# Two PSUM banks for the turned probabilities, one for the values, and the value product last in each head

## The reference, cut to what matters

```python
# experts: each token sums the rows of its 8 experts
g = out_pad[eid, slot] * (w.reshape(-1) * valid.astype(w.dtype))[:, None]
y = jnp.zeros((T, Hd), x.dtype).at[tok].add(g)
...
# attention, per batch and head (4 x 16)
scores = jnp.einsum('bhtd,bhsd->bhts', q, k) / scale
attn = jax.nn.softmax(jnp.where(mask, scores, -jnp.inf), axis=-1)
out = jnp.einsum('bhts,bhsd->bhtd', attn, v)
return out.transpose(0, 2, 1, 3).reshape(B, T_text, N_HEADS * HEAD_DIM) @ Wo
...
# feed-forward, per batch
h = jax.nn.silu(bitlinear158(x, w1, b1))
h = jax.nn.gelu(h, approximate=False)
h = layer_norm(h, ln_g, ln_b)
return bitlinear158(h, w2, b2)
```

## Time and profile before

| | us |
|---|---|
| three runs | 549.42, 546.50, 547.52 |
| median | 547.52 |
| the profiled execution | 546.43 |
| its span from first to last instruction | 544.5 |
| slot loop, first `scores` to last `project` | 256.6 to 513.3 |
| tail behind it | 513.3 to 544.5 |
| busy over the span | PE 485.3 (89%), DVE 436.0 (80%), ACT 393.5 (72%), POOL 246.4 (45%) |

### The profile page before, as it was taken

The page is one execution under the profiler, slowest core; times in us unless marked ns, Lnnn a source line. Parts: engine busy times, 40 slices in busy tenths (PEclk is TensorE's granted clock), DMA queues, the critical chain, the costliest instruction groups (busy, mean ns, idle before and its releaser), DMA issues.

```text
span 544.5 us, 10844 instructions
## 1 busy us (share of the span) xinstructions
PE 485.3 (89%) x3402; PEld 399.9 (73%) x3402; DVE 436.0 (80%) x1213; ACT 393.5 (72%) x928; POOL 246.4 (45%) x255
## 2 busy tenths in 40 slices
PE   8958888799997999998999999987999889997925
PEld 6445555666787677777899999976999789986804
DVE  4889999999968487986668559869888699766887
ACT  2786777585374567886877777898687997798654
POOL 1139999894106656302772376125861232122121
PEclk9958999899999999998999999999899999999867
DMA  6655887572788997925220034001660000000000
GB/s 178 152 173 176 230 272 225 173 220 78 206 256 244 291 316 213 301 92 194 59 69 2 17 77 59 7 2 17 77 82 3 2 1 1 22 1 0 2 20 19
DMA packets 52558, 61.65 MB, mean 113 GB/s; under 512 B 6284, under 2 KB 42742, under 8 KB 52502
## 3 DMA queue, kind: packets, MB, share of 16 engines
q1 hardware_dynamic: 48662, 49.43, 30.5%
q0 software_dynamic: 3840, 11.54, 10.0%
HBM read 54.27 MB, written 6.69 MB: 112 GB/s over the span
## 4 chain that ended last, share of the span: by engine, by line
PE 49%; issue 17%; DVE 14%; ACT 12%; POOL 6%; DMA 2%; DVEq 0%; SPq 0%; ACTq 0%; POOLq 0%
PE ps L1712 8%; PE ps L1650 7%; PE ps L1651 6%; PE ps L1652 6%; DVE hst L1968 4%; PE ps L1701 4%; PE ps L1568 3%; PE ps L1370 2%; ACT pr L1085 2%; POOL dbu L636 2%; DVE hc L1980 2%; PE ps L1604 2%; PE ps L1589 2%; POOL G L683 1%; PE ps L1378 1%
## 5 line engine op out<-in xcount | busy, mean ns | idle before, releaser
L636 POOL TENSOR_TENSOR dbu<-du,brow 128x512 f32<-128x512 f32 x64 | 82.4, 1324 | 22.3 <-DVE du L1955 18.7
L721 POOL TENSOR_TENSOR pn<-pr,pinv 128x256 f32<-128x256 f32 x64 | 40.9, 639 | 107.8 <-DVE pinv L2376 107.3
L1712 PE MATMUL ps<-pT,cS 128*128 128x256 f32 x256 | 67.4, 386 | 0.0
L1085 ACT ACTIVATE pr<-ebuf,smin 128x256 f32<-128x256 f32 x128 | 63.6, 501 | 2.4 <-issue 1.8
L872 ACT ACTIVATE ps<-dtv,amat 128x510 f32<-128x510 f32 x64 | 44.0, 695 | 24.4 <-DVE hst L1968 19.5
L683 POOL DMA_INDIRECT G<-token_rows,idx_x x32 | 37.8, 1180 | 43.1 <-DVE wkv L2104 20.8
L705 POOL DMA_INDIRECT G<-expert_out,idx_g x48 | 50.9, 1061 | 11.5 <-issue 11.1
L2366 DVE CUSTOM_DVE_ANT_0 ebuf<-ps,mbias 128x256 f32<-128x256 f32 x128 | 49.0, 420 | 2.6 <-issue 2.6
L1650 PE MATMUL ps<-xnT,mqk 128*128 128x256 f32 x128 | 47.2, 368 | 4.3 <-DVE qT L2336 2.5
L1701 PE MATMUL ps<-ident,pn 128*128 128x128 f32 x256 | 39.5, 277 | 9.2 <-ACT pT L1100 5.0
L1712 PEld LDWEIGHTS ps<-pT,cS 128*128 128x128 f32 x256 | 44.8, 193 | 3.9
(11 more groups left out here) (387 smaller groups left out, 1486.2 us busy)
## 6 DMA issues: line engine op xcount, KB each, us to landing
brow<-state_rows SPq DMA_DIRECT2D x16, 512.0 KB, 4.0
wdn<-in_L_ffn_wd SPq DMA_DIRECT2D x12, 384.0 KB, 6.7
ebuf<-state_rows SPq DMA_DIRECT2D x17, 256.0 KB, 5.4
wgu<-in_L_ffn_wg SPq DMA_DIRECT2D x11, 384.0 KB, 5.3
wgu<-in_L_ffn_wu SPq DMA_DIRECT2D x11, 384.0 KB, 7.3
expert_out<-xn SPq DMA_DIRECT2D x11, 256.0 KB, 4.3
wo<-in_L_xattn_Wo SPq DMA_DIRECT2D x4, 512.0 KB, 5.8
wq<-in_L_xattn_Wq SPq DMA_DIRECT2D x4, 512.0 KB, 5.7
```

The source lines that it names most:

```text
L636: nc.gpsimd.tensor_tensor(dbu[:, j, :], du[:, j % 2, at:at + 512], brow[:, pair % BRING, j // 2, :], ALU.mult).then_inc(pool_dbu, 1)
L1085: last = A(pr[:, h % 2, tt, :], sneg[:, h % 2, tt, :], ACT.Exp, scale=-1.0, bias=smin[:, h % 2, tt:tt + 1], accum_out=psum_[:, h % 2, tt:t ...
L1712: last = pe.matmul(ps[:, 3 + 2 * (h % 2), 0:L], cS[:, b % 2, st, :], pT[:, h % 2, st, :], start=(st == 0), stop=(st == 1))
```

## The change

1. **Banks.** `turn_p` writes bank 4 for even heads and bank 5 for odd ones, and so waits for `turned_p` of two heads back instead of one. `values` writes one half or the other of bank 3, and so waits for `o_low` of the head just before it instead of two back.
2. **Order within a head.** On PE `values` goes behind `queries` and `project`, to the end of the slot. On ACT `o_high` goes behind `exps`. On DVE `o_low` goes behind `q_low`.
3. **Feed-forward.** `gelu` 1 is set apart from `gelu` 0: for f = 0 and 1 from at 13 (late) to at 14 (ACT's third place), for f = 2 from ahead of `q_high` to behind it. `squares` 1 of f = 0 and 1 goes behind `q_high`. `normal_hidden` 1 goes to the late place for f = 0 and 1, and `normal_hidden` 0 of f = 2 too.
4. **Gathers.** One at h = 0, two each at h = 1 to 7, one at h = 8.

```diff
@@ -434,6 +434,9 @@
         def query_out(i):
             return ps[:, 5 if i == 1 else 0, 0:L]
 
+        def values_out(h):
+            return ps[:, 3, L * (h % 2):L * (h % 2) + L]
+
         def cols(ap, a, b):
             return ap[:, a:b]
 
@@ -763,26 +766,28 @@
                 if b + 1 < B:
                     if h == 0:
                         gather(b + 1, 0, 0)
+                    if h == 1:
                         gather(b + 1, 0, 1)
                         gather(b + 1, 0, 2)
-                    if h == 1:
+                    if h == 2:
                         gather(b + 1, 0, 3)
                         gather(b + 1, 0, 4)
-                    if h == 2:
+                    if h == 3:
                         gather(b + 1, 0, 5)
-                    if h == 3:
                         gather(b + 1, 0, 6)
+                    if h == 4:
                         gather(b + 1, 0, 7)
-                    if h == 4:
                         gather(b + 1, 1, 0)
+                    if h == 5:
                         gather(b + 1, 1, 1)
+                        gather(b + 1, 1, 2)
                     if h == 6:
-                        gather(b + 1, 1, 2)
                         gather(b + 1, 1, 3)
                         gather(b + 1, 1, 4)
                     if h == 7:
                         gather(b + 1, 1, 5)
                         gather(b + 1, 1, 6)
+                    if h == 8:
                         gather(b + 1, 1, 7)
                     if h == 12:
                         root3(b + 1)
@@ -1097,13 +1102,13 @@
                 i = NH * b + h
                 act.wait_ge(pT_in_psum, i + 1)
                 wait_count(act, av_done, i - 1)
-                A(pT[:, h % 2].rearrange("p a b -> p (a b)"), bank(4), ACT.Copy).then_inc(pT_ready, 1)
+                A(pT[:, h % 2].rearrange("p a b -> p (a b)"), bank(4 + h % 2), ACT.Copy).then_inc(pT_ready, 1)
 
             def o_high(b, h):
                 i = NH * b + h
                 act.wait_ge(av_done, i + 1)
                 wait_count(act, o_added, i - 1)
-                A(oT[0][:, h % 2], bank(3 + 2 * (h % 2))[:, 0:L], ACT.Copy).then_inc(o_hi, 1)
+                A(oT[0][:, h % 2], values_out(h), ACT.Copy).then_inc(o_hi, 1)
 
             def preload(at, function):
 
@@ -1205,18 +1210,19 @@
                         silu(f, 1)
                     if at == 12 and f == B - 2:
                         gelu(f, 0)
-                        gelu(f, 1)
-                    if at == 18 and f < B - 2:
-                        squares(f, 1)
                     if at == 22 and f < B - 2:
                         turned_hidden(f, 0)
                     if at == (22 if f < B - 2 else 20):
                         turned_hidden(f, 1)
-                if 4 <= slot < NH * B + 4:
-                    o_high((slot - 4) // NH, (slot - 4) % NH)
                 if slot + 2 < NH * B:
                     q_high((slot + 2) // NH, (slot + 2) % NH)
                 for f, at in feeds(slot):
+                    if at == 14 and f < B - 2:
+                        gelu(f, 1)
+                    if at == 12 and f == B - 2:
+                        gelu(f, 1)
+                    if at == 18 and f < B - 2:
+                        squares(f, 1)
                     if at == 8 and f == B - 2:
                         turned(f)
                     if at == 13 and f == B - 2:
@@ -1231,6 +1237,8 @@
                     normal_half((slot - 1) // NH, (slot - 1) % NH)
                 if slot < NH * B:
                     exps(b, h)
+                if 4 <= slot < NH * B + 4:
+                    o_high((slot - 4) // NH, (slot - 4) % NH)
                 if slot == NH * B:
                     preload(1, ACT.Gelu)
                 if b + 1 < B:
@@ -1695,10 +1702,10 @@
                 i = NH * b + h
                 pe.wait_ge(p_ready, i + 1)
                 pe.wait_ge(p_half, i + 1)
-                wait_count(pe, pT_ready, i)
+                wait_count(pe, pT_ready, i - 1)
                 for st in range(2):
                     for tt in range(2):
-                        last = pe.transpose(ps[:, 4, L * st + P * tt:L * st + P * tt + P],
+                        last = pe.transpose(ps[:, 4 + h % 2, L * st + P * tt:L * st + P * tt + P],
                                             pn[:, h % 2, tt, P * st:P * st + P], ident[:])
                 last.then_inc(pT_in_psum, 1)
 
@@ -1707,9 +1714,9 @@
                 pe.wait_ge(pT_ready, i + 1)
                 if h == 0:
                     pe.wait_ge(rows_ready, b + 1)
-                wait_count(pe, o_ready, i - 1)
+                wait_count(pe, o_ready, i)
                 for st in range(2):
-                    last = pe.matmul(ps[:, 3 + 2 * (h % 2), 0:L], cS[:, b % 2, st, :], pT[:, h % 2, st, :], start=(st == 0),
+                    last = pe.matmul(values_out(h), cS[:, b % 2, st, :], pT[:, h % 2, st, :], start=(st == 0),
                                      stop=(st == 1))
                 last.then_inc(av_done, 1)
 
@@ -1826,12 +1833,12 @@
                 for f, at in feeds(slot):
                     if at == 9 and f == B - 2:
                         into(f, 0)
-                if 4 <= slot < NH * B + 4:
-                    values((slot - 4) // NH, (slot - 4) % NH)
                 if slot + 2 < NH * B:
                     queries((slot + 2) // NH, (slot + 2) % NH)
                 if 5 <= slot < NH * B + 5:
                     project((slot - 5) // NH, (slot - 5) % NH)
+                if 4 <= slot < NH * B + 4:
+                    values((slot - 4) // NH, (slot - 4) % NH)
                 if b + 1 < B:
                     if h == 13:
                         turn_xn3(b + 1)
@@ -2379,7 +2386,7 @@
                 i = NH * b + h
                 dve.wait_ge(o_hi, i + 1)
                 wait_count(dve, o_added, i - 1)
-                low(oT[1][:, h % 2], bank(3 + 2 * (h % 2))[:, 0:L], oT[0][:, h % 2], o_ready)
+                low(oT[1][:, h % 2], values_out(h), oT[0][:, h % 2], o_ready)
 
             def add_attention(b):
                 dve.wait_ge(o_added, NH * b + NH)
@@ -2743,10 +2750,8 @@
                         centred(f, 0)
                     if at == 15 and f == B - 2:
                         centred(f, 1)
-                    if at == (17 if f < B - 2 else 15):
+                    if at == 17 and f < B - 2:
                         normal_hidden(f, 0)
-                    if at == 17 and f < B - 2:
-                        normal_hidden(f, 1)
                     if at == (18 if f < B - 2 else 16):
                         largest(f, 0)
                     if at == 17 and f == B - 2:
@@ -2757,10 +2762,10 @@
                         scaled(f)
                     if at == 19 and f == B - 2:
                         scale_round(f, 1)
+                if slot + 2 < NH * B:
+                    q_low((slot + 2) // NH, (slot + 2) % NH)
                 if 4 <= slot < NH * B + 4:
                     o_low((slot - 4) // NH, (slot - 4) % NH)
-                if slot + 2 < NH * B:
-                    q_low((slot + 2) // NH, (slot + 2) % NH)
                 if b + 1 < B:
                     if h == 6:
                         add_choices(b + 1, 0, 0)
@@ -2793,6 +2798,8 @@
                         variance(f)
                         centred(f, 1)
                     if at == 15 and f == B - 2:
+                        normal_hidden(f, 0)
+                    if at == (17 if f < B - 2 else 15):
                         normal_hidden(f, 1)
                     if at == 18 and f < B - 2:
                         largest(f, 1)
```

## The result

| | us | ratio to before |
|---|---|---|
| before, median of 4 runs (546.50 to 549.42) | 547.49 | |
| after, median of 4 runs (563.73 to 567.92) | 565.36 | 1.0337, 95% interval 1.0305 to 1.0370 |
| forecast | 556.5 (549 to 562) | 1.016 |

A forecast was written before the change was run, and what follows sets the result against it. PE was taken to bound plain heads, and ACT the heads with feed-forward work from its gelu on. Terms 5.1 + 1.9 + 0.4 + 2.0 = 9.4 us on 546.43 gave 555.8, forecast as 556.5, range 549 to 562.

The forecast's parts named there:

- Plain heads at 3.43: Heads without feed-forward work stay at PE's own 3.43 us each, costed at nothing, with 0.7 us of cover for `project`.
- f = 1, +5.1: Slots 40 to 53 take 61.7 us instead of 56.65, from per-head rings summing to 59.0 plus 0.29, 0.86 and 1.56.
- The rings: One chain per head over ACT and DVE: `o_high`, `o_low`, reciprocal, mask, exponentials; 2.62 us, late DVE work added in full.
- f = 0, +1.9: Slots 24 to 37: same rings as f = 1, gathers hidden beneath them, set against 59.84 us.
- The 3.2 us between f = 0 and f = 1: 59.84 against 56.65 us for the same 14 slots, put down to gathers; slot 35 began 1.90 late on POOL's `pn`.
- Batch boundary, +0.4: At slot 14 `queries` waits 0.7 us instead of 0.3 for the next rows' low part; later two boundaries lie inside rings.
- the walk: Ring lengths added up slot by slot for f = 1 and from slot 60 on; chance 0.62 (552 to 559).
- Gathers too late for the sums, the last rival: A batch's last gather moves from slot 7 to 8; sums wanting it end slot 9, some 7 us on: hidden; no chance given.
- Two banks: Two banks for turned probabilities: all 5.0 us of `turn_p` waits on ACT's copy go, but turn into waits for `o_low`.
- End of the loop, +2.0: From slot 60 to the last `project`: 30.7 us instead of 28.7, by rings and the last three heads at 2.6 each.
- a rival for the mid-loop waits: Three PE waits over 3 us each bring a stretch at 1.2 GHz, +1 to +2 each: 559 to 562, chance 0.08.
- one doubt (what overlaps): Whether `project`'s waits overlap others: at best sum +2.6 (549 to 550); at worst none overlap, tail heads 3.4 each (+12).

The follow-up runs named there:

- the extra pass: One more DVE pass in slots 16 to 19, run in both kernels: slots 14 to 23 took 34.44 us before (34.44 without), 36.18 in the new (34.87 without).
- the two kernels of the last windows above: The kernel before (547.5 us), then it with gathers spread and new feed-forward places of f = 0 and 1 alone, old banks and order: 544.91 us, 0.9952.

## Why the prediction was right in direction and half in size

- *Plain heads at 3.43:* right, 3.44, and the extra pass shows how near the edge they are.
- *f = 1, +5.1:* +5.7, mostly as walked. The rings sum to 0.2 less than forecast, `add_attention` adds 0.86. The row for it was in the trace of before (0.74 us of DVE behind `q_low` at that slot) and has no term in the sum.
- *f = 0, +1.9:* +3.1. The same 0.86; two rings were 0.2 and 0.4 longer than in f = 1, the second by a pass of DVE that took 1.12 instead of 0.74. The 3.2 us between f = 0 and f = 1, put down to gathers, are not all theirs: with the gathers spread and the old order f = 0 still takes 1.2 longer.
- *Batch boundary, +0.4:* +0.4 in the stretch of slots 14 to 23, in part by luck. Slot 14 is 0.34 longer; slot 21, the first `project` of the batch, adds 0.23, and the other heads, at 3.41 instead of 3.43, give 0.14 back.
- *Slots 54 to 59, no term:* +0.4. Slot 57 took 5.92 instead of 5.39: late feed-forward work of f = 2 stands in the rings there too, and the walk began at slot 60.
- *Gathers too late for the sums, the last rival:* it was called hidden and is not quite. In slot 9 a sum waited 0.60 us for the last gathers, behind `o_low` and so in the ring:

```profile
288.68 1.29 DVE L2307 TENSOR_TENSOR G<-G 128x512 f32<-128x512 f32 x2 [0.60 <-DMA G<-expert_out,idx_g]
```

  The stretch of slots 6 to 13 is 0.7 longer; with the old order and the old banks the same wait was 1.03 us and cost nothing, but with the old order and the new banks (1.10 us) slot 11 took 3.97 instead of 3.43.
- *Two banks:* the rule on banks that the prediction set against its rings (the Trainium skill, PSUM — Partial Sum Buffer, Summary: rules for kernel authors) gives no gain here: 1.0024 alone. The wait for the copy was real, but PE then waited elsewhere: the 5.0 us gave way to 11.1 us of `values` waiting for `o_low`. In the new order the list of waits has none of `values` for `o_low`: there, as the prediction had it, `project` stands just ahead with the same wait.
- *End of the loop, +2.0: this is the step that failed.* It is +6.0. The price of four rings was right (7.32, 3.54, 3.25, 5.02 against 7.6, 3.55, 3.25, 5.0). Missed were the start (1.19, from PE's lead), a copy that the move of `o_high` put ahead of the last head's (1.5), the handoffs of the last rings (0.4) and the clock (1.1 in one ring). The clock stood in the prediction as a rival for the mid-loop waits at +1 to +2; there the clock stayed at 1.00 behind waits of 2.54 and 2.56 us, and it fell at the end of the loop, which had no such term.
- *The range* took the worst case from one doubt (what overlaps) and not from the term with the least evidence. The rings of the end of the loop had been walked once, without the table of which ACT and DVE instruction now stands on which side of `o_high` and `o_low`.

In the traces +15.5 us are accounted for. The medians differ by 17.9; the other 2.4 are not explained by a row. They are of the size by which executions of one kernel differ (563.7 to 567.9); the traces show two things that vary so, the part ahead of the loop and how often the clock falls.

## What to carry to other kernels

A step moved behind another on one engine and ahead of the late work on a second may close a loop over both: add up that loop once per iteration, and set it against the bound engine's own time; work that was free beside it is then paid in full. After moving a step, list for every place, the last iterations above all, which other instructions have changed sides with it, and who waits for them. A wait removed on an engine that isn't the limit can come back as another wait of the same engine, and was worth nothing here.

## What the runs showed of the hardware

- In the new kernel PE's clock fell to 0.50 behind a wait of 3.16 us (slot 61) and stayed at 1.00 behind waits of 2.54 and 2.56 (slots 31 and 47). The length of the wait alone doesn't settle it. In the kernel before it fell behind the 1.90 us of slot 35, and with the DVE passes added, which lie far ahead of it, the same wait of 1.90 us left it at 1.00. Each of the two kernels of the last windows above waited 1.89 us for `o_low` in slot 64; it fell in the first and not in the second.
- Filling the waits of slots 31, 47 and 61 with idle transposes moved the fall to the next long wait, in slot 65; with 61 and 65 filled the end of the loop was free of it. That same trace has half-clock stretches in slots 30 and 46, behind waits of 1.70 us, where the new kernel had none; they cost nothing that shows (62.95 and 62.36 us against 62.89 and 62.32).
- The same pass of `scale_round` took 1.12 us in f = 0 and 0.74 in f = 1. In f = 0, POOL's `pn` had begun 0.06 before it and ran to 391.81; in f = 1 POOL did nothing meanwhile. DVE in both, and POOL in f = 0:

```profile
391.25 1.12 DVE L2532 TENSOR_SCALAR wgu<-wgu,fqs 128x1024 f32<-128x1024 f32 x1
...
462.53 0.74 DVE L2532 TENSOR_SCALAR wgu<-wgu,fqs 128x1024 f32<-128x1024 f32 x1
```

```profile
391.19 0.62 POOL L724 TENSOR_TENSOR pn<-pr,pinv 128x256 f32<-128x256 f32 x1
391.97 1.32 POOL L708 DMA_INDIRECT G<-expert_out,idx_g  x1 [0.16 <-issue]
```

  Other traces shift the two against each other. Where `pn` had begun 0.04 to 0.07 us ahead (eight traces, of the new kernel and of kernels made from it), the pass took 1.12 to 1.14; where it had begun 0.56 to 0.57 ahead and was all but done (six), 0.74 to 0.75. Where `pn` began 0.46 or 0.47 behind the pass (three), both were longer, the pass 0.95 or 0.96 and `pn` 0.95 or 0.96 instead of 0.62. The Trainium skill (SBUF — State Buffer, SBUF: two separate sides) says that a POOL instruction and a DVE instruction in a 2-port mode, or one that reads two operands from SBUF, lock each other out: the one that starts first keeps the shared ports to its end. Whether this pass is in such a mode no row says. By that rule it would be 0.56 us late in f = 0, and it was 0.38 longer, so the sense agrees and the size doesn't; and in the three traces the pass, though first, was 0.21 longer too, which the rule doesn't give (a gather of POOL had also begun ahead of it there).
